# A decoder layer's second pass: TensorE's order inside a row, score tiles between whole products

## What is computed

```python
x = _layernorm(x + mamba(x))                       # first pass of the kernel
# second pass, both parts below:
q, k, v = x @ Wq.T + bq, ctx @ Wk.T + bk, ctx @ Wv.T + bv      # 16 heads of 32, 77 keys
x = _layernorm(x + softmax(mask(q k^T / sqrt(32))) v @ Wo.T + bo)
xr = mu_r * x + (1 - mu_r) * x_prev                # x_prev: one position earlier
xk = mu_k * x + (1 - mu_k) * x_prev
x = _layernorm(x + sigmoid(xr @ W_r) * (relu(xk @ W_k)**2 @ W_v))
```

## Time and profile before

| | us |
|---|---|
| time, median of 3 runs | 2580.58 (2575.85 to 2581.28) |
| profiled execution, its own time | 2579.53 |
| its span | 2577.7 |
| PE busy | 2409.9 (93%) |
| DVE / POOL / ACT busy | 1822.4 / 1668.7 / 1475.5 |

### The profile page before, as it was taken

How to read it: one execution, slowest core, us unless ns; L and a number is a source line. 1 busy time by engine, 2 the same in 40 slices (tenths; PEclk the granted TensorE clock), 3 DMA queues, 4 the chain that set the end, 5 groups by cost and what they waited for, 6 DMA issues and landing times. The chain is left out here.

```text
span 2577.7 us, 38451 instructions
## 1 busy us (share of the span) xinstructions
PE 2409.9 (93%) x15488; PEld 1426.6 (55%) x15488; DVE 1822.4 (71%) x2154; ACT 1475.5 (57%) x2258; POOL 1668.7 (65%) x912
## 2 busy tenths in 40 slices
PE   6899999999999999999999989877999999999997
PEld 3466566656566666656656666544445554554543
DVE  2898798798798799789889879841465355456443
ACT  2587577677678678667757867631333443333332
POOL 0698899888899889879988989951333134133130
PEclk8899999999999999999999999988999999999998
DMA  3777978977978987897897797755000010000000
GB/s 125 202 162 161 239 162 173 245 162 167 234 164 180 207 196 165 177 232 156 179 238 156 166 223 151 168 107 202 1 17 17 33 33 1 33 33 1 17 17 17
DMA packets 158832, 342.75 MB, mean 133 GB/s; under 512 B 39232, under 2 KB 102208, under 8 KB 127808
## 3 DMA queue, kind: packets, MB, share of 16 engines
q0 software_dynamic: 27648, 201.34, 39.7%
q1 hardware_dynamic: 131008, 138.97, 16.4%
HBM read 119.57 MB, written 19.37 MB: 54 GB/s over the span
## 5 line engine op out<-in xcount | busy, mean ns | idle before, releaser
L898 POOL TENSOR_TENSOR mamba_ring<-mamba_ring,mamba_c_row 128x1024 f32<-128x1024 f32 x512 | 1277.0, 2627 | 66.4 <-DVE mamba_ring L789 65.0
L789 DVE TENSOR_TENSOR_SCAN mamba_ring<-mamba_ring,ps 128x512 f32<-128x512 f32 x1024 | 1180.5, 1203 | 188.6 <-PE ps L381 187.7
L635 ACT ACTIVATE mamba_ring<-mamba_delta,mamba_a_neg 128x512 f32<-128x512 f32 x1024 | 661.1, 711 | 102.9 <-DMA mamba_ring<-mamba_ring 101.7
L381 PEld LDWEIGHTS ps<-mamba_diag_b,mamba_v_t 64*128 64x128 f32 x8192 | 503.2, 189 | 321.9 <-issue 244.2
L381 PE MATMUL ps<-mamba_diag_b,mamba_v_t 64*128 64x128 f32 x8192 | 594.2, 285 | 34.6 <-DVE mamba_ring L789 33.8
L296 PE MATMUL ps<-mamba_xt,mamba_wu 128*128 128x512 f32 x512 | 254.9, 626 | 33.8 <-DMA mamba_wu<-w_u 16.9
L907 POOL DMA_DIRECT2D mamba_ring<-mamba_ring x192 | 179.4, 934 | 139.6 <-DMA mamba_ring<-mamba_ring 102.3
L349 PE MATMUL ps<-mamba_xt,mamba_wres 128*128 128x512 f32 x512 | 256.6, 619 | 0.0
L1552 POOL TENSOR_TENSOR xf_pr<-xf_pr,xf_top 128x1232 f32<-128x1232 f32 x32 | 75.0, 2343 | 275.7 <-DVE xf_top L1470 275.7
L402 PE MATMUL ps<-mamba_ident,mamba_ring 128*128 128x128 f32 x1024 | 145.9, 289 | 40.4 <-DMA mamba_ring<-mamba_ring 40.4
L1545 POOL TENSOR_TENSOR xf_xn<-xf_xn,xf_bo_s 128x512 f32<-128x512 f32 x32 | 39.5, 1267 | 222.2 <-PE xf_ps L1122 222.2
(11 more groups left out here) (116 smaller groups left out, 2904.1 us busy)
## 6 DMA issues: line engine op xcount, KB each, us to landing
mamba_ring<-mamba_ring POOLq DMA_DIRECT2D x192, 1024.0 KB, 7.8
mamba_c_row<-c_rows SPq DMA_DIRECT2D x32, 1024.0 KB, 15.5
mamba_wu<-w_u SPq DMA_DIRECT2D x64, 256.0 KB, 3.3
mamba_wres<-w_res SPq DMA_DIRECT2D x64, 256.0 KB, 6.1
mamba_diag_b<-b_diagonals SPq DMA_DIRECT2D x56, 256.0 KB, 14.2
mamba_xt<-x_t SPq DMA_DIRECT2D x8, 1024.0 KB, 15.8
mamba_xres<-x SPq DMA_DIRECT2D x32, 256.0 KB, 8.3
x<-mamba_xres SPq DMA_DIRECT2D x32, 256.0 KB, 5.1
```

The lines of the kernel that those rows point to most:

```text
L381: m = nc.tensor.matmul(ps[:, 2 * s + i, tb * P:(tb + 1) * P], v_t[g % 2][i * H:(i + 1) * H, tb * P:(tb + 1) * P], diag_b[i * H:(i + 1) * H ...
L635: a = nc.scalar.activation(ring[:, q % NR, i, :], delta[:, d % EARLY, :], ACT.Exp, scale=a_neg[:, d, 2 * k + i:2 * k + i + 1])
L789: m = nc.vector.tensor_tensor_scan(ring[:, r, i, :], ring[:, r, i, :], both[:, bass.ds(i, T, 2)], 0.0, ALU.mult, ALU.add)
L898: nc.gpsimd.tensor_tensor(ring[:, q % NR], ring[:, q % NR], c_row[:, 2 * k:2 * k + 2, :], ALU.mult).then_inc(c_done, 1)
```

## The change

In rows b > 0 PE's order becomes: q products, k 0, scores 0, k 1, scores 1, k 2, scores 2, k 3, r 0, scores 3, r 1 to 3, `ffn_v`. Row 0 keeps its order. `ffn_k` no longer goes through `product_a`: its first product waits before each slice for that slice's mix, where a single wait for all four stood before; that holds for the tail too. The orders of DVE, ACT, POOL and SP are not touched.

```diff
-            def ffn_k(a, j):
-                product_a(a, KT + j, lambda kt: wkf_s[:, kt, j * P:(j + 1) * P], lambda kt: xk[:, kt, :])
+            def ffn_k(b, a, j):
+                a_bank(a + (KT + j + 1))
+                for kt in range(KT):
+                    if j == 0:
+                        pe.wait_ge(mixed, b * (2 * KT) + kt + 1)
+                    m = nc.tensor.matmul(ps[:, (a + j) % 4, :], wkf_s[:, kt, j * P:(j + 1) * P], xk[:, kt, :],
+                                         start=(kt == 0), stop=(kt == KT - 1))
+                m.then_inc(a_filled, 1)
...
                 q_product(b, 2)
                 q_product(b, 3)
-                scores(b, 0)
                 if b > 0:
                     a = ffn_a(b - 1)
-                    pe.wait_ge(mixed, (b - 1) * (2 * KT) + KT)
-                    ffn_k(a, 0)
-                    ffn_k(a, 1)
-                else:
-                    k_context(1, 0)
-                    k_context(1, 1)
-                scores(b, 1)
-                if b > 0:
-                    ffn_k(a, 2)
-                    ffn_k(a, 3)
-                else:
-                    k_context(1, 2)
-                    k_context(1, 3)
-                scores(b, 2)
-                scores(b, 3)
-                if b > 0:
+                    for tb in range(TT - 1):
+                        ffn_k(b - 1, a, tb)
+                        scores(b, tb)
+                    ffn_k(b - 1, a, KT - 1)
                     pe.wait_ge(mixed, (b - 1) * (2 * KT) + 2 * KT)
-                    for tb in range(TT):
+                    ffn_r(a, 0)
+                    scores(b, TT - 1)
+                    for tb in range(1, TT):
                         ffn_r(a, tb)
                     ffn_v(b - 1, scores_v(b) + TT * KT)
                 else:
+                    scores(b, 0)
+                    k_context(1, 0)
...
             x2_transposes(NB - 1)
-            pe.wait_ge(mixed, NB * (2 * KT) - KT)
             for j in range(KT):
-                ffn_k(LAST_A, j)
+                ffn_k(NB - 1, LAST_A, j)
```

More of the change, by code:

```diff
@@ L1270, in row @@
                 else:
+                    scores(b, 0)
+                    k_context(1, 0)
+                    k_context(1, 1)
+                    scores(b, 1)
+                    k_context(1, 2)
+                    k_context(1, 3)
+                    scores(b, 2)
+                    scores(b, 3)
                     for i in range(VB, NB):
```

## The result

The changed kernel takes 2561.34 us in the median of six executions against 2580.09 before, also of six now (ratio 0.9931, 95% interval 0.9917 to 0.9944): faster by 0.7%, 18.7 us by the medians and 17.8 by the ratio, where 23 were forecast. One of the six took 4792.96 us; it is left out of the ratio, no row here explains it, and without it the median is 2561.08. The profiled execution took 2562.99 us.

A forecast was written before the change was run, and what follows sets the result against it. PE, busy 93%, was taken as the bound, with waits and clock falls around the scores. Rows 21.2, less 1.9 for clock, plus tail 2.0 and 1.6: 22.9 off 2579.53, plus 1.05 for the median, 2557; 8-in-10 range 2550 to 2570.

The forecast's parts named there:

- Scores 2 and 3 apart: PE, rows 1 to 7: separating these runs removes 0.51 and 1.17 us of waiting and 1.9 of slow r products.
- Scores 2 wait in their place: PE, row 3: scores 2 must wait for DVE to empty the banks of scores 1, running 2075.53 to 2077.80.
- The clock: PE's granted clock in the seven rows: one fall booked, 1.9 us; bounds none (0) and one in each (13.3).
- The choice between two distant rows: New scores 2, 2.3 us of tiles, judged nearer to 0.77 idle plus 1.1 tiles (no fall) than 3.9 (falls).
- The rival that more alternation of tiles and whole products lowers the clock: PE, seven rows: falls at scores 1, 2 and 3 cost 39.9 us, making the kernel slower, 2596; chance 4%.
- PE's own work: PE, row 3: products and scores walked anew with 0.18 us a switch; r1 to r3 end at 2096.45.
- POOL and DVE: Row 3: POOL's last squares end at 2096.50, together with PE, so `ffn_v` starts 34.0 us after q's end.
- centring 3 stands at 3.11 behind DVE's take ... The lag is gone there: POOL, row 3: centring 3 starts at 2089.6, as usual after DVE's take, so earlier lateness no longer counts.
- The lag of centring 2: POOL, row 3: squares 0 and 1 go first, so centring 2 starts at 2085.1 and not 2083.94.
- the lag could survive to the squares: Rival, DVE and POOL bound the rows earlier: 1.1 us a row, 7.7 less gain, 2565; chance 10%.
- Tail: Last row's k products: start 2.0 us earlier by slice waits, plus 1.6, half of 3.1 lost to low clock.
- the 0.77 before scores 0: PE, rows 1 to 7: wait for ACT's take of q, to vanish behind the first k product.

The follow-up runs named there:

- split_only: Kernel before with only r product 0 put between scores 2 and scores 3: 2562.11 us, ratio 0.9931 to the kernel before.
- joined: Changed kernel with scores 2 and 3 side by side again, between k 3 and r 0: 2572.07 us, ratio 0.9979 to the kernel before.
- dense_tiles: Changed kernel with POOL's squares behind centring 3 and scores 1 computed three times over: 2559.14 us, ratio 0.9928 to the kernel before.
- pool_order: Changed kernel with POOL's squares of all four k products behind centring 3, ahead of weigh 2: 2551.34 us, ratio 0.9891 to the kernel before.

## Why the prediction was right, and where it was off

- *Scores 2 and 3 apart* (0.51 and 1.17 of waiting, 1.9 and more of slow r products a row): right, and more than the whole gain of the rows. Scores 3 and r are as walked, and split_only and joined show it from both sides.
- *Scores 2 wait in their place*, 2075.53 to 2077.80 forecast, 2.27: measured 2.27.
- *The clock*: one fall in seven rows was booked, 1.9 us; there was none. The choice between two distant rows was right in direction, by choice and not by a working. What lowers it is now bounded more closely: one run of scores spread over 2.3 us does not (changed kernel); 2.9 of dense ones do not (dense_tiles); 1.1 of dense ones, 0.5 to 1.1 idle and 2.3 or more thinly spaced do (before, joined). Idle time, thin spacing and the length of the whole stretch were not parted from each other. The rival that more alternation of tiles and whole products lowers the clock did not come: 1.00 in all seven rows.
- *PE's own work*, with 0.18 for a switch: walked to end 33.9 behind q's end, measured 33.7 (2081.16 + 10.57 less 2058.07).
- *POOL and DVE*: the step that failed; the time still fell in the range. I had `ffn_v` at 34.0 behind q's end, on "centring 3 stands at 3.11 behind DVE's take ... The lag is gone there". The lag of centring 2 was right (1.1 forecast, 1.3 measured), but I let it die inside POOL's list. It reached DVE, by the scaling step that took 2.22 and not 0.98. So 34.81, 0.8 a row, 5.7 in all, and the wait that this made cost another 1.9 (the 0.27 of drain and weight load, seven times). The rival "the lag could survive to the squares" (1.1 a row) came nearly whole (7.7 in its sum, 7.6 here), though not by way of POOL's list alone, as the forecast had it.
- *Tail*: 2.0 forecast for the earlier start, 1.7 measured; 1.6 for the clock, 1.2 measured. The second is not a property of the gap: with the same gap of 2.2, k took 13.97 (joined), 15.67 (five kernels) and 16.71 (two). What decides among these was not tried.

From the sum: 22.9 forecast, less 7.6 (5.7 and 1.9), plus 1.9 for the fall that did not come, less 0.7 in the tail, is 16.5, the difference of the spans. The medians differ by 18.7; the other 2 lie in no row of the second pass and are less than the first pass scatters, so that the median came nearer to the forecast than the rows did is luck, and so is that the fall booked in vain made up for part of the wait.

The forecast also took the 0.77 before scores 0 as gained, and never asked what the new order would give without it, since the walk took the change whole. PE does save the 0.77, but scores 0 start later by a k product, DVE's late mixes pass the delay on, and it comes back as PE's wait for the squares: by split_only the k products' place costs 0.9 a row in this kernel.

## What to carry to other kernels

When PE's order changes, walk the other engines' lists with the new times, and where two engines' instructions newly overlap, look whether one of them ends each time with the other: a duration in the trace (0.98, 4.72) may be a wait in disguise and grow. A stretch in which PE idles and works thinly can cost as much again through the clock: here 1.7 us of waiting a row brought 1.9 and more of slow products behind it, and putting one whole product between the two runs removed both. And before putting work ahead of a stage, see that what the stage feeds isn't already late: here four mixes moved on DVE were worth about as much again as the change (18 us by the pitch of the rows, some 12 by the ratios).

## What the runs showed of the hardware, unexpected

- A DVE instruction on 16 numbers a partition took 2.22 us because POOL's centring ran, and 0.18 with no POOL instruction beside it; four mixes took 4.72 beside a centring and 2.84 without it.
- The wait of PE for the squares cost, beside its idle 1.15 us, another 0.27 (rows 1.42 longer than pool_order's): 0.17 of drain that nothing overlapped and 0.10 for the next weight load (14.00 against 13.90).
- Dense 32-row tiles, 96 instructions in 2.9 us, keep TensorE at 2.4 GHz; two runs of such tiles over 3.9 us, with half an idle us between and the second thinly spaced, lose it. Whether it is the idle time, the spacing or the length stays open.
